# A layer norm applied by ScalarE and a causal mask added by VectorE, in an attention and expert kernel

## The reference, cut to what matters

```python
x = x + tanh(g_xattn[0]) * xattn(layernorm(x), ctx)     # 16 batches of 512 tokens, 256 wide
x = x + tanh(g_ffn[0]) * experts(layernorm(x))
# xattn: q, k, v of 16 heads, 16 wide each; only the first 512 context tokens can be seen
scores = q @ k.T / 4
scores = where(tril(512 x 512), scores, -inf)
y = softmax(scores) @ v ; return y @ Wo.T + bo
# experts: softmax of 8 logits a token, top 128 tokens an expert and batch, silu(gate) * up, down, added in
# layernorm(x) = (x - mean) / sqrt(var + 1e-5)
```

## Time and profile before

| | |
|---|---|
| median of 3 runs | 1925.38 us (1925.32 to 1926.35) |
| the profiled execution's own time | 1929.9 us |
| its span, first to last instruction | 1928.1 us |
| busy: PE, PEld, DVE, ACT, POOL | 92%, 55%, 58%, 45%, 48% of the span |
| mean granted TensorE clock | 0.976 |
| busy in a steady 50 us of attention (300 to 350 us): PE, DVE, ACT, POOL | 48.3, 42.5, 30.3, 36.6 us |

### The profile page before, as it was taken

How to read it: one execution, slowest core, us unless ns; L and a number is a source line. 1 busy time by engine, 2 the same in 40 slices (tenths; PEclk the granted TensorE clock), 3 DMA queues, 4 the chain that set the end, 5 groups by cost and what they waited for, 6 DMA issues and landing times.

```text
span 1928.1 us, 41223 instructions
## 1 busy us (share of the span) xinstructions
PE 1781.3 (92%) x13350; PEld 1052.6 (55%) x13414; DVE 1112.6 (58%) x2777; ACT 871.7 (45%) x1684; POOL 922.4 (48%) x963
## 2 busy tenths in 40 slices
PE   3799999999999999963899999999999999999997
PEld 1355555555555555531456565655655665656565
DVE  2678888888888888736743434343434344343431
ACT  1356555665655655632343434343334334343332
POOL 4467777777777776544143332424232424233322
PEclk9799999999999999986999999999999999999999
DMA  6676777777777776439365673645646645445222
GB/s 150 155 166 165 182 184 186 186 186 186 185 181 183 186 183 153 118 93 230 82 112 88 120 124 86 103 88 102 111 68 127 117 84 101 86 87 89 50 32 24
DMA packets 411285, 247.66 MB, mean 128 GB/s; under 512 B 293271, under 2 KB 392735, under 8 KB 411167
## 3 DMA queue, kind: packets, MB, share of 16 engines
q1 hardware_dynamic: 386591, 212.53, 47.6%
q0 software_dynamic: 24576, 33.57, 11.0%
HBM read 118.63 MB, written 58.72 MB: 92 GB/s over the span
## 4 chain that ended last, share of the span: by engine, by line
PE 49%; DVE 2%; SPq 1%; DMA 1%; issue 1%; POOL 1%; ACT 0%; POOLq 0%
PE bank L1090 11%; PE bank L1089 11%; PE bank L1091 10%; PE bank L1107 6%; PE bank L1106 6%; PE bank L1105 6%; SPq L1016 1%; DMA gate_raw<-in_L_ffn_w_gate 1%; DVE h L1207 0%; DVE h L1210 0%; ACT h L1135 0%; SPq L995 0%; DVE top_at L1157 0%; POOL gate_nat L1034 0%; POOL up_nat L1034 0%
## 5 line engine op out<-in xcount | busy, mean ns | idle before, releaser
L1055 POOL DMA_INDIRECT out<-y,row_now x128 | 202.0, 1578 | 604.7 <-ACT y L1142 580.0
L579 ACT ACTIVATE prob<-bank 128x512 f32<-128x512 f32 x640 | 367.6, 598 | 230.2 <-PE bank L472 146.7
L1207 DVE TENSOR_TENSOR h<-bank,silu 128x512 f32<-128x512 f32 x256 | 176.3, 689 | 395.7 <-PE bank L1091 262.8
L662 DVE CUSTOM_DVE_ANT_0 masked<-bank,causal 128x384 bf16<-128x384 f32 (+1 forms) x512 | 300.4, 616 | 51.5 <-PE bank L449 49.5
L1135 ACT ACTIVATE h<-h 128x512 bf16<-128x512 f32 x256 | 161.7, 632 | 345.7 <-DVE h L1207 330.1
L449 PE MATMUL bank<-ks,qs 96*128 96x128 bf16 (+3 forms) x1024 | 277.1, 306 | 37.2 <-DVE mx L662 15.1
L1210 DVE TENSOR_TENSOR h<-h 128x512 bf16<-128x512 f32 x256 | 177.3, 693 | 179.9 <-ACT h L1135 176.3
L1107 PE MATMUL bank<-downT,h 128*128 128x256 bf16 x1024 | 279.1, 273 | 0.0
L1105 PE MATMUL bank<-downT,h 128*128 128x256 bf16 x1024 | 279.1, 273 | 0.0
L1106 PE MATMUL bank<-downT,h 128*128 128x256 bf16 x1024 | 279.1, 273 | 0.0
L1090 PE MATMUL bank<-tokT,gateT 128*128 128x512 bf16 x511 | 194.7, 381 | 35.2 <-DMA tokT<-rows 29.1
(11 more groups left out here) (144 smaller groups left out, 2832.7 us busy)
## 6 DMA issues: line engine op xcount, KB each, us to landing
q_parts<-q_sb SPq DMA_DIRECT2D x64, 192.0 KB, 2.9
k_parts<-k_sb SPq DMA_DIRECT2D x64, 192.0 KB, 3.3
qs<-q_parts SPq DMA_DIRECT2D x64, 192.0 KB, 3.0
ks<-k_parts SPq DMA_DIRECT2D x64, 192.0 KB, 3.3
x_t<-in_x SPq DMA_DIRECT2D x16, 512.0 KB, 3.9
ctx_t<-in_ctx SPq DMA_DIRECT2D x16, 512.0 KB, 4.7
qs<-q_parts SPq DMA_DIRECT2D x64, 128.0 KB, 2.9
ks<-k_parts SPq DMA_DIRECT2D x64, 128.0 KB, 3.3
```

The lines of the kernel that those rows point to most:

```text
L579: nc.scalar.activation(prob[:, gr % 2, h0:h0 + nh, POFF[tiles[0]]:POFF[tiles[0]] + w], sc_bank[SC_BANK[k]][:, 0:nh * w].rearrange("p (h w) ...
L662: nc.vector.tensor_tensor_reduce(masked[:, k % 2, 0:w], max_bank[max_at(gr, k)][:, 0:w], causal[:, T - w:T], 1.0, LOWEST, ALU.add, ALU.max ...
L1055: nc.gpsimd.indirect_dma_start(out_rows, bass.IndirectOffsetOnAxis(ap=row_now[:, par, c, s:s + 1], axis=0), y[:, c % 2, s, :], None, compu ...
```

## The change

It does four things. The mask matmuls of units 0 to 2 go, with `identb`, `mask_qk` and their preparation. DVE takes the maximum of units 0, 1 and 2 with the masking instruction too, once for each head (4, 2 and 2 instructions in place of 1, 1 and 1). The pieces "ln1+" and "ln2+" go from DVE to ACT, at the same places of the list, as Identity(rstd * x + shift) with rstd and shift as per-partition operands. POOL makes shift = -mean * rstd in two more instructions of 128 x 4 elements behind each power; DVE waits with the next batch's bn_aggr until shift of the batch before is made.

```diff
@@ attention, tensor
-                            ks[0:STACK, gr, h0 + h, 0:w], start=True, stop=nh == 1)
-                        if nh > 1:
-                            last = nc.tensor.matmul(dst[:, h * w + w - P:(h + 1) * w], identb[:, :], mask_qk[:, :],
-                                                    start=False, stop=True)
+                            ks[0:STACK, gr, h0 + h, 0:w], start=True, stop=True)
@@ attention, scalar
+                elif kind in ("ln1+", "ln2+"):
+                    n, half = kind[:-1], p[2]
+                    if n == "ln1":
+                        wait(act, split_lo["x"], count(b, 2, 0))
+                    else:
+                        wait(act, filled["xt"], count(b, 2, 0))
+                        wait(act, tok_lo, count(b, 1, 0))
+                    wait(act, ln_shift[n], count(b, 1, 1))
+                    dst, src = (xn, x_t) if n == "ln1" else (xn2, x1)
+                    for i in (2 * half, 2 * half + 1):
+                        nc.scalar.activation(dst[:, i, :], src[:, i, :], ACT.Identity, bias=shift[n][:, i:i + 1],
+                                             scale=rstd[n][:, i:i + 1]).then_inc(ln_done[n], 1)
@@ attention, vector
+                wait(dve, ln_shift[n], count(b, 1, 0))
                 wait_apart(dve, ln_stats[n], count(b, NT, NT), passed["dve"])
...
-            def norm_apply(n, dst, src, b, half):
-                wait(dve, ln_rstd[n], count(b, 1, 1))
-                for i in (2 * half, 2 * half + 1):
-                    nc.vector.tensor_scalar(dst[:, i, :], src[:, i, :], mean_var[n][:, i, 0:1],
-                                            rstd[n][:, i:i + 1], ALU.subtract, ALU.mult).then_inc(ln_done[n], 1)
...
-                    if nh == 1:
-
-                        wait(dve, max_read, n - 1)
-                        wait_apart(dve, max_filled, n + 1, passed["dve"])
-                        nc.vector.tensor_tensor_reduce(
-                            masked[:, k % 2, 0:w], max_bank[max_at(gr, k)][:, 0:w], causal[:, T - w:T], 1.0, LOWEST,
-                            ALU.add, ALU.max, mx[:, gr % 2, h0, i:i + 1]).then_inc(max_read, 1)
-                        return
-                    wait(dve, max_filled, n + 1)
-                    nc.vector.tensor_reduce(mx[:, gr % 2, h0:h0 + nh, i], max_bank[max_at(gr, k)][
-                        :, 0:nh * w].rearrange("p (h w) -> p h w", h=nh), AX.X, ALU.max).then_inc(max_read, 1)
+                    wait(dve, max_read, n - 1)
+                    wait_apart(dve, max_filled, n + 1, passed["dve"])
+                    for h in range(nh):
+                        part = slice(h * w, (h + 1) * w)
+                        last = nc.vector.tensor_tensor_reduce(
+                            masked[:, (gr * NMAX + k) % 2, part], max_bank[max_at(gr, k)][:, part], causal[:, T - w:T], 1.0, LOWEST,
+                            ALU.add, ALU.max, mx[:, gr % 2, h0 + h, i:i + 1])
+                    last.then_inc(max_read, 1)
@@ attention, gpsimd, behind the power
+                    nc.gpsimd.tensor_tensor(out=shift[kind][:, :], in0=mean_var[kind][:, :, 0], in1=minus_one[:, :],
+                                            op=ALU.mult).then_inc(ln_minus[kind], 1)
+                    wait(pool, ln_rstd[kind], count(b, 1, 1))
+                    wait(pool, ln_minus[kind], count(b, 1, 1))
+                    nc.gpsimd.tensor_tensor(out=shift[kind][:, :], in0=shift[kind][:, :], in1=rstd[kind][:, :],
+                                            op=ALU.mult).then_inc(ln_shift[kind], 1)
```

More of the change, by code:

```diff
@@ L173, in flamingo @@
         ident = sb(stack, "ident", [P, P], F32)
-        identb = sb(stack, "identb", [P, P], BF16)
         aff = sb(stack, "aff", [P, NT, BATCH * EXPERTS], F32)
@@ L186, in attention @@
     x, ctx_kv, out = g["x"], g["ctx_kv"], g["out"]
-    ident, identb, aff, tanh_g, passed = g["ident"], g["identb"], g["aff"], g["tanh_g"], g["passed"]
+    ident, aff, tanh_g, passed = g["ident"], g["aff"], g["tanh_g"], g["passed"]
     max_bank, sc_bank, pv_bank, job_bank = g["max_bank"], g["sc_bank"], g["pv_bank"], g["job_bank"]
     q_dram, k_dram, tok_dram = g["q_dram"], g["k_dram"], g["tok_dram"]
-    mask_qk = sb(ctx, "mask_qk", [P, P], BF16)
     causal = sb(ctx, "causal", [P, T], F32)
@@ L231, in attention @@
     rstd = {n: sb(ctx, f"{n}_rstd", [P, NT], F32) for n in ("ln1", "ln2")}
+    shift = {n: sb(ctx, f"{n}_shift", [P, NT], F32) for n in ("ln1", "ln2")}
+    minus_one = sb(ctx, "minus_one", [P, NT], F32)
     lmax = sb(ctx, "lmax", [P, NT, 1], F32)
@@ L243, in attention @@
     w_loaded = {n: sem(f"{n}_loaded") for n in ("wq", "wk", "wv", "wo", "gate_w")}
-    gates_loaded, consts, cast, turned, hi_taken, evac, tanh_done, bias_done, tails, tails_made = (
-        sem(n) for n in ("gates_loaded", "consts", "cast", "turned", "hi_taken", "evac", "tanh_done", "bias_done", "tails",
+    gates_loaded, consts, turned, hi_taken, evac, tanh_done, bias_done, tails, tails_made = (
+        sem(n) for n in ("gates_loaded", "consts", "turned", "hi_taken", "evac", "tanh_done", "bias_done", "tails",
                          "tails_made"))
     order = [(n, o) for n in ("wq", "wk", "wv", "wo") for o in range(NH2)]
-    CONSTS = 9
+    CONSTS = 8
     TAILS = 32
@@ L280, in attention @@
     ln_rstd = {n: sem(f"{n}_rstd_done") for n in ("ln1", "ln2")}
+    ln_minus = {n: sem(f"{n}_minus_done") for n in ("ln1", "ln2")}
+    ln_shift = {n: sem(f"{n}_shift_done") for n in ("ln1", "ln2")}
     ln_done = {n: sem(f"{n}_done") for n in ("ln1", "ln2")}
@@ L429, in _ @@
             pe.wait_ge(evac, n + 1)
-            pe.wait_ge(cast, 1)
             def piece(body, p):
@@ L709, in piece @@
                     norm_stats("ln1", x_t, b, p[2])
-                elif kind == "ln1+":
-                    wait(dve, split_lo["x"], count(b, 2, 0))
-                    norm_apply("ln1", xn, x_t, b, p[2])
                 elif kind == "ln2":
@@ L715, in piece @@
                     norm_stats("ln2", x1, b, p[2])
[L716 to L720, removed]
                 elif kind == "lt+":
@@ L742, in _ @@
             dve.wait_ge(consts, CONSTS)
-            nc.vector.tensor_copy(identb[:, :], ident[:, :]).then_inc(cast, 1)
             piece(-1, ("ln1", 0, 0))
@@ L829, in _ @@
             nc.gpsimd.memset(ident[:, :], 0.0).then_inc(consts, 1)
-            nc.gpsimd.memset(mask_qk[:, :], 0.0).then_inc(consts, 1)
             nc.gpsimd.memset(gwT[:, :, EXPERTS:32], 0.0).then_inc(consts, 1)
             nc.gpsimd.memset(minus_half[:, :], -0.5).then_inc(consts, 1)
+            nc.gpsimd.memset(minus_one[:, :], -1.0).then_inc(consts, 1)
             nc.gpsimd.memset(v_aug[:, :, :, :], 1.0).then_inc(consts, 1)
@@ L838, in _ @@
             nc.gpsimd.affine_select(out=ident[:, :], in_=ident[:, :], compare_op=ALU.not_equal, fill=1.0,
-                                    base=0, pattern=[[-1, P]], channel_multiplier=1).then_inc(consts, 1)
-            nc.gpsimd.affine_select(out=mask_qk[:, :], in_=mask_qk[:, :], compare_op=ALU.is_ge, fill=NEG,
                                     base=0, pattern=[[-1, P]], channel_multiplier=1).then_inc(consts, 1)
```

## The result

The changed kernel takes 1970.51 us (median of 5 runs, 1969.07 to 1974.75), the kernel before, run beside it, 1926.35 us (1925.32 to 1928.94). The ratio is 1.0222, 95% interval 1.0208 to 1.0236: slower by 44 us. The prediction said 1890 us, 1866 to 1914. The profiled execution has a span of 1973.0 us against 1928.1.

What follows compares the result with a forecast made beforehand. PE was taken as the bound, DVE close behind; 2.4 us a body over 15 bodies, 36 us, less about 1 at attention's end, took 1929.9 to 1895, and the median, 4.5 lower, to 1890 us; range 1866 to 1914.

Steps and rivals of the forecast that it cites:

- DVE, maxima: Masking instructions for units 0 to 2 on DVE: 0.36 us more a group, 1.4 us a body.
- One more masked buffer turn, the constants and the cast at the start: Extra setup at the start of the kernel: below 1 us once, hidden by weight loads.
- rival A: DVE's short masking instructions cost their full time, leaving 0.9 us a body won: 1912 us; chance 0.14 with milder forms.
- milder form: Each short masking instruction on DVE costs 0.05 us more than forecast: 1897 us.
- rival B: POOL's multiplications cost as much as the power, so nearly all the gain is given back: 1922 us; chance 0.06.
- rival C: ACT loads a table of 1.28 us around each switch to Identity: 1995 us; chance 0.08, shared with other ACT queue stalls.
- what was worked out for group 0: ACT's first pair stands between exponentials 2 and 3, so PE waits at sc of unit 5: 0.55 us lost.
- They count except where PE runs into a wait: Mask matmuls removed from PE's path: 0.48 us a group, 1.9 us a body.
- group 1's 0.60: PE's late start of group 1, 0.60 us, was to vanish as DVE loses 2.23 us of work in group 0.

Runs made afterwards that it cites:

- after_shifted: The changed kernel, DVE's loop kept, with 64 semaphore increments issued once ahead of that loop: 1911.62 us.
- after_straight: The changed kernel with DVE's bodies 3 to 13 written out in place of its hardware loop, the other engines keeping their loops: 1912.11 us.
- ln_only: The changed kernel with mask matmuls and reductions as before, so only layer norms on ACT and shift on POOL remain changed: 1916.88 us.

## Why the prediction was wrong, point by point

**The step that failed** is one that is not there. "DVE, maxima" priced the instructions by their time and never counted them as code; "One more masked buffer turn, the constants and the cast at the start: below 1 us once" was the whole account of what is not work; and among the rivals for slower stood a load of ACT's tables, not one of instructions. The stall costs 1970.5 - 1911.6 = 59 us, over ten jumps back 5.9 us each: 4.4 to 5.3 us of DVE's idle time, of which PE stands 3.4 to 4.3, and after it 3.4 or 6.8 us of PE at 0.50 of the full clock. Without it the kernel would be at 1911.6, inside the range I gave but 22 us above its middle.

**Right, part by part.** The masking instruction's steps are 0.21 us at 128 columns (402.07 to 402.29) and 0.34 to 0.35 at 256, for 0.20 and 0.34; rival A, full times, is out, and so is its milder form of 0.05 us more each: no run shows the 0.05, the steps came at most 0.01 us above the forecast. POOL's multiplications take 0.198 and 0.199 us, for 0.18; rival B is out. ACT's pair takes two steps of 0.49 us for my 0.46 (instructions of 586 ns for 560); that SBUF as the source adds a little shows in the kernel before, where ACT copies 128x512 in 616 ns out of SBUF (L1123) and in 582 to 597 out of PSUM (L605). There is no further table load, as the trace of the changed kernel has two in all, the same as before: rival C is out. The first pair of ACT does what was worked out for group 0. PE of after_shifted:

```profile
381.70 0.33 PE L450 MATMUL bank<-ks,qs 96*128 96x384 bf16 x1
382.44 0.23 PE L467 MATMUL bank<-qs,ks 128*128 128x128 bf16 x1 [0.41 <-ACT prob L577]
```

0.41 shown and 0.16 of pipe are 0.57 us of loss at sc of unit 5, for 0.55 forecast.

**Mis-sized: the masks.** "They count except where PE runs into a wait" was the right sentence, and then I counted them nearly everywhere, 1.9 us a body. They are worth 0.3. The groups of after_straight against those of before show where: group 0 won 0.23 us (forecast 0.74), group 1 0.08 (0.43), groups 2 and 3 together 0.88 (1.25). In all 1.2 of 2.4, and the body without the stall is 47.8, where 46.5 was forecast.

**Wrong: "DVE loses 2.23 us of work in this group and is no longer late: group 1's 0.60 comes back."** The work went, but what follows on DVE hangs on PE, not on DVE's queue. DVE of after_shifted:

```profile
383.77 0.08 DVE L667 DVE_READ_ACCUMULATOR2_ANT mx<- 128x1 f32 x1
384.83 0.75 DVE L706 SCALAR_TENSOR_TENSOR x<-bank,tanh_g,res_t 128x512 f32<-128x512 f32 x1 [0.98 <-PE bank L526]
385.50 0.55 DVE L667 CUSTOM_DVE_ANT_0 masked<-bank,causal 128x384 bf16<-128x384 f32 x1
...
387.45 0.68 DVE L667 CUSTOM_DVE_ANT_0 masked<-bank,causal 128x512 bf16<-128x512 f32 x1
...
388.67 0.68 DVE L667 CUSTOM_DVE_ANT_0 masked<-bank,causal 128x512 bf16<-128x512 f32 x1
...
389.28 0.28 DVE L667 CUSTOM_DVE_ANT_0 masked<-bank,causal 128x128 bf16<-128x128 f32 x1
```

The time saved ahead of the o projection's sum became 0.98 us of idle time there, and behind it the long units follow each other at 0.61 us as before, up to the start of group 1. The slack gained before this wait for PE was not carried over it.

**Right in direction:** the norms off DVE win time (0.9 us a body by themselves, ratio 0.9943), and a longer slow start is not to be seen: the clock from 50 to 100 us is 0.84 in after_straight and after_shifted, against 0.80.

The version to keep is after_shifted, which beats both kernels: 0.9921 (0.9906 to 0.9936) of the time before, with the loop kept. after_straight does the same, at the price of ten more bodies of DVE code; ln_only gets 0.9943; with 228 instructions its loop can't lie in four pieces, so by the argument above (not tried at other places) it is safe wherever it stands.

## What to carry to other kernels

Where an engine runs a hardware loop, count its instructions before and after a change, not only their time, and look at the instruction queue of the page and for "issue" behind the jump: here 55 instructions more cost nothing at one place of the code and 46 to 59 us at another, and a few idle instructions ahead of the loop, or the loop written out, get it back. Two versions of a kernel whose loops are near such a length cannot be compared until both are free of the stall. And a matmul taken off the busiest engine is worth its time only as far as the engines close behind it have room: 1.5 us of steps gave 0.3.

## What was not expected of the hardware

- A loop of 296 instructions on DVE (18.9 KB of code) runs with no fetch in one place and with five 8 KB packets and a gap of 4.3 to 5.3 us a turn in another, 30 or 64 instructions away; 241 instructions ran free at both places tried.
- After 3.7 us without a matmul PE ran at 0.50 of full clock for about 6 us (3.4 us behind three of the ten gaps), a second loss of the same stall (steps of 0.10 us for 128 columns, 403.35 to 403.45, in place of 0.06).
- The masking instruction's cost is nearly linear down to 128 columns: steps of 0.21, 0.345, 0.47 and 0.61 us at 128, 256, 384 and 512.
